# One maximum over 1024 keys instead of two over 512, and two banks of scores instead of three, in an attention kernel

## The chip, the cores and the metric

The kernel runs on one core of a Trainium2 chip. The metric is the time of one execution on the device in microseconds (us), as the median of several runs. The core has engines that run side by side and wait for one another by semaphores: TensorE (PE in the profile; its weight loads are PEld), VectorE (DVE), ScalarE (ACT), GpSimd (POOL) and SyncE (SP), which issues most of the transfers.

## What is computed

The input is 16 images of 128 channels by 32 x 32. Each image is normalised over its channels, read as 1024 tokens of 128 numbers, and goes through attention with 8 heads of size 16; the result is added to the image. Then the tokens go through a mixture of 16 experts of which each token takes two. The change touches the attention alone:

```
xs = reshape(_ln_c(x), (B, T, C))                 # B = 16, T = 1024, C = 128
q, k, v = per head xs @ Wq[h], xs @ Wk[h], xs @ Wv[h]
scores = einsum('bhtd,bhsd->bhts', q, k) * scale
att = softmax(scores, axis=-1)                    # over 1024 keys
out = einsum('bhts,bhsd->bhtd', att, v) ... @ Wproj + bproj
x = x + out
```

The softmax needs the maximum of each query's 1024 scores before the exponentials.

## The kernel before, in words

An image is worked on in 4 stages (2 groups of 4 heads, 2 halves of 512 queries). A stage has 32 slots, so an image has SLOTS = 128, numbered u in the code. In each slot TensorE does two things of the same size. `max_unit` (line 1265) multiplies 128 queries of one head by one half of the keys, 512 columns, into a bank of `ps_max`; a unit m has kh = m % 2 for the half of the keys, so an even unit and the odd one behind it belong to the same queries. VectorE takes the maximum over those columns (`take_max`, line 843), and in the first slot of the next stage `row_maxima` (line 850) joins the two halves. `split_m` writes the negated maximum as two bf16 parts (lines 864, 866, 869); TensorE turns them into rows (`rows_of_maxima`, line 1274), ScalarE copies these (`copy_m`, line 732), and a transfer puts them beside the queries. `score_unit` (line 1287) then computes the scores again, transposed, 128 keys by 512 queries with the maximum already subtracted, into a bank of `ps_score`; ScalarE takes the exponential (`exp_unit`, line 706) into `probs`; `weigh` (line 1306) multiplies by the values into `ps_pv`.

The maxima run LEAD = 46 units ahead of the scores, so before the first score stand 46 maxima, and in slot u TensorE does maximum u + 46 and score u. In an even slot the maximum comes first, in an odd slot the score, so that two scores stand next to each other. Weighing comes behind odd slots, by a table WEIGH_AT: at 1 and 3, then 7, 8, 9, 11 and every odd slot to 31 of a stage; none comes behind slot 5 of a stage.

PSUM has 8 banks of 512 fp32 columns. Three hold scores, three hold maxima (RING = 3), one holds the weighed values and one, `misc`, everything else. A unit may be written to a bank when its reader is through: score u waits for `exp_done`, maximum m for `max_taken`, both by `ring_free`, which means the third unit back. All orders are written out by hand and every engine takes its instructions in order. Beside the main work the slots hold the neighbouring images' other work: TensorE transposes the next image in slots 1 and 5, projects its queries and keys in 29, 41, 44, 48 and its values in 51 and 54; it projects the output of the last image in 13 and 17, transposes tokens in 22 and 24, does the logits in 36 and counts the tokens of each expert in 100. ScalarE copies what these give, and has `copy_xt` behind exponentials 2 and 6 (line 712), `copy_m` in slot 27 of each stage and `copy_rows` (line 749) behind exponentials 76 and 80. VectorE has `divide` in slots 4 to 7 of each stage (transposes and the division of the weighed values), statistics of the next image in 8 to 15 and of the last in 24 to 31, residual additions in 13 and 17, and steps of the choice of experts from 44 on. GpSimd adds the bias to the residual (line 544). SyncE stacks the parts of queries and keys for the next image (`stack`, line 325, twelve transfers) once score 63 is done; the maxima of the next image begin with unit 128, in slot 82, and wait for them. Images 1 to 14 are turns of a loop; the first and the last are written out.

Of the kernel before, what the change touches and what calls it, by code (L numbers as in the profile page):

```python
# [8 lines left out]
ALU = mybir.AluOpType  # L9
ACT = mybir.ActivationFunctionType  # L10
AX = mybir.AxisListType

P = 128
# [5 lines left out]
HALF = T // 2  # L19
# [4 lines left out]
STAGES = G * 2  # L24
UNITS = TB * HG
SLOTS = STAGES * UNITS
LEAD = 46
MSLOT = 26
RING = 3
PRING = 16  # L30
NORMS = 14
BUSY = (3, 4, 5, 6, 7, 18, 19, 20, 21)
# [9 lines left out]
STACK = 16 * len(Q_PART)  # L42
# [20 lines left out]
def wait(eng, sem, value):  # L63

    if isinstance(value, int) and value <= 0:
        return
    eng.wait_ge(sem, value)
# [10 lines left out]
def ring_free(n):  # L78


    return n - RING + 1 if n % SLOTS >= SLOTS % RING else n - SLOTS % RING + 1

# [6 lines left out]
def metaformer(nc, x, wq, wk, wv, wproj, bproj, wgate, w1, w2, out):  # L89
    ctx = ExitStack()  # L90
    with ctx:
        def sb(name, shape, dt=FP32):
            return ctx.enter_context(nc.sbuf_tensor("sb_" + name, shape, dt))

        def sem(name):
            return ctx.enter_context(nc.semaphore(name))
# [18 lines left out]
        qs, ks = stacks[:, 0], stacks[:, 1]  # L115
# [33 lines left out]
        blk_dest = arena_d[:, XR * ROWW + (WR + 2) * P:XR * ROWW + (WR + 2) * P + WR].bitcast(I32)  # L149
        o_t = sb("o_t", [P, HALF // 32, 32])  # L150
        o_rec = sb("o_rec", [P, HALF // 32])
        m_red = sb("m_red", [P, 2, UNITS])
        m_neg = sb("m_neg", [P, 2, HG * HG])
        m_rest = sb("m_rest", [P, HG * HG])
        m_parts = sb("m_parts", [P, HG, MPARTS, HG], BF16)
# [49 lines left out]


        banks = ctx.enter_context(nc.psum_tensor("banks", [P, 8, HALF], FP32))
        ps_score, ps_max = banks[:, 0:RING], banks[:, RING:2 * RING]
        ps_pv, misc = banks[:, 6], banks[:, 7]
        ps_h, ps_o, ps_xt = banks[:, 0:2], banks[:, 2:4], banks[:, 6:8]  # L210
        ps_y = banks[:, 0:4].rearrange("p (s h) t -> p s h t", s=2)
# [20 lines left out]
        v_placed = sem("v_placed")  # L232
        max_ready = sem("max_ready")
        max_taken = sem("max_taken")
        m_ready = sem("m_ready")
        m_split = sem("m_split")
        m_psum = sem("m_psum")
        m_copied = sem("m_copied")
# [599 lines left out]
        def _(dve):  # L838
            def take_max(b, m):

                s, u = m // UNITS, m % UNITS
                wait(dve, max_ready, SLOTS * b + m + 1)
                nc.vector.tensor_reduce(out=m_red[:, s % 2, u:u + 1], in_=ps_max[:, m % SLOTS % RING, :], axis=AX.X,  # L843
                                        op=ALU.max).then_inc(max_taken, 1)

            def row_maxima(b, s):
                k = STAGES * b + s
                wait(dve, max_taken, UNITS * (k + 1))
                wait(dve, m_split, 3 * (k - 1))
                nc.vector.tensor_reduce(out=m_neg[:, s % 2, :],  # L850
                                        in_=m_red[:, s % 2, :].rearrange("p (n s) -> p n s", s=2),
                                        axis=AX.X, op=ALU.max, negate=True).then_inc(m_ready, 1)

            def split_m(b, s, step):

                k = STAGES * b + s
                neg = m_neg[:, s % 2, :].rearrange("p (t h) -> p t h", t=HG)
                rest = m_rest[:, :].rearrange("p (t h) -> p t h", t=HG)
                wait(dve, m_split, 3 * k + step)
                if step == 0:  # L860
                    wait(dve, m_ready, k + 1)

                    wait(dve, m_psum, k)
                    nc.vector.tensor_copy(m_parts[:, :, 0, :], neg).then_inc(m_split, 1)
                if step == 1:
                    nc.vector.tensor_tensor(out=rest, in0=neg, in1=m_parts[:, :, 0, :],
                                            op=ALU.subtract).then_inc(m_split, 1)
                if step == 2:
                    nc.vector.tensor_copy(m_parts[:, :, 1, :], rest).then_inc(m_split, 1)
# [153 lines left out]
            for o in range(2):  # L1023
# [6 lines left out]
                                    op=ALU.subtract).then_inc(setup_v, 1)  # L1030
# [4 lines left out]
            for i in range(4):  # L1035
                o, half = i // 2, i % 2
# [4 lines left out]
                for level in (1, 2):  # L1041
                    dve.wait_ge(qk_parts, 5 * i + 2 * level - 1)
                    nc.vector.tensor_tensor(out=f, in0=f, in1=parts[:, o, level - 1, cols],
                                            op=ALU.subtract).then_inc(qk_parts, 1)
                    dve.wait_ge(qk_parts, 5 * i + 2 * level)
                    nc.vector.tensor_copy(parts[:, o, level, cols], f).then_inc(qk_parts, 1)
            for m in range(LEAD):
                take_max(0, m)
                if m == UNITS:
                    row_maxima(0, 0)  # L1050
                if 0 < m - UNITS < 4:
                    split_m(0, 0, m - UNITS - 1)

            def batch(b, first, last):
                for u in range(SLOTS):
                    m = u + LEAD
                    if not (last and m >= SLOTS):
                        take_max(b, m)
                    if m % UNITS == 0 and not (last and m > SLOTS):
                        row_maxima(b, m // UNITS - 1)  # L1060
                    if 0 < m % UNITS < 4 and not (last and m > SLOTS + 4):
                        split_m(b, m // UNITS - 1, m % UNITS - 1)
                    if 4 <= u % UNITS < 8 and not (first and u < UNITS):
                        divide(b, u // UNITS - 1, u % UNITS - 4)
                    if not last:
                        if 8 <= u < 16:
                            norm_stats(b + 1, 0, xt_copied, ln1_stats, u - 8)
                        if u == 17:
                            norm_means(b + 1, 0, ln1_stats)
                    if not first:  # L1070
                        if u == 13:
                            add_residual(b - 1, 0)
                        if u == 17:
                            add_residual(b - 1, 1)
                        if 24 <= u < 32:
                            norm_stats(b - 1, 1, tok_copied, ln2_stats, u - 24)
                        if u == 32:
                            norm_means(b - 1, 1, ln2_stats)
                        if u == 38:
                            choose(b - 1)  # L1080

                        if u == 44:
                            choice = choose_experts(b - 1)
                        if u >= 44 and u % 2 and u % UNITS not in BUSY:
                            next(choice, None)

            batch(0, True, False)
            with dve.Fori(1, B - 1) as b:
                batch(b, False, False)
# [30 lines left out]
            def three(t):  # L1120
# [9 lines left out]
                                        op=ALU.is_le))  # L1130
# [95 lines left out]
        def _(pe):  # L1226
# [29 lines left out]
            def max_unit(b, m):  # L1256

                s, u = m // UNITS, m % UNITS
                bb = b + s // STAGES
                g, half = s % STAGES // 2, s % 2  # L1260
                h, t, kh = u // 8, u // 2 % 4, u % 2
                if u == 0 and half == 0:
                    wait(pe, stacked[g], 192 * (bb + 1))
                wait(pe, max_taken, SLOTS * b + ring_free(m))
                nc.tensor.matmul(ps_max[:, m % SLOTS % RING, :], qs[0:STACK, g, h, half * HALF + t * P:half * HALF + (t + 1) * P],  # L1265
                                 ks[0:STACK, g, h, kh * HALF:(kh + 1) * HALF], start=True,
                                 stop=True).then_inc(max_ready, 1)

# [252 lines left out]
```

## Time and profile before

| | |
|---|---|
| median of 3 runs | 2675.8 us (2669.5 to 2680.6) |
| span of the profiled execution | 2676.3 us |
| TensorE matmuls | 2423.1 us busy, 91% |
| VectorE | 1997.1 us busy, 75% |
| ScalarE | 1511.7 us busy, 56% |
| GpSimd | 1187.5 us busy, 44% |
| mean granted clock of TensorE | 0.958 of full speed |

The profile is of one execution. Its span runs from the first to the last instruction. A busy share is a mean over stages with different limits: attention lasts to about 1942 us, the experts take the rest, and only in attention does the change have a part. A matmul's record is longer than the distance to the next one, since matmuls overlap; it is the distance between starts that tells the pace. In a timeline "x2" is two instructions in a row merged, and the bracket behind a row gives the idle time before it and what ended it.

### The profile page before, as it was taken

What the parts mean: (1) busy time and instruction counts of PE and PEld (TensorE: products, weight loads), DVE (VectorE), ACT (ScalarE), POOL (GpSimd) and SP (SyncE); (2) the same over time, 40 slices, a digit from 0 to 9 for tenths busy, and PEclk for the clock granted to TensorE, in tenths of its full rate; (3) what the DMA queues carried; (4) which work ended last, traced back from release to release, by engine and by line L of the source; (5) the groups of instructions that cost most, each with busy time, mean ns of one, the idle gap of its engine ahead of it and who ended that gap; (6) DMA issues with size and microseconds to landing.
All of it is one profiled execution on the core that took longest, in us unless ns stands there. A gap on an engine that the chain in (4) does not pass through costs nothing. (4 is left out here: it accounts for less than half of the span.)

```text
span 2676.3 us, 67960 instructions
## 1 busy us (share of the span) xinstructions
PE 2423.1 (91%) x18706; PEld 1203.4 (45%) x18706; DVE 1997.1 (75%) x4671; ACT 1511.7 (56%) x2881; POOL 1187.5 (44%) x1833
## 2 busy tenths in 40 slices
PE   3999999999999999999999999999928999999963
PEld 1333333333333333333333333333318999999962
DVE  6888888978888888888888898889624555555544
ACT  0576666766667666666666676667703444444420
POOL 4304536363544536263543637354264444444430
PEclk9999999999999999999999999999959999999985
DMA  2233222223232222223222222322062222222249
GB/s 44 33 52 55 51 42 59 34 58 53 57 59 48 59 34 58 41 58 65 53 51 42 58 34 58 63 47 57 10 179 62 63 63 63 63 64 63 63 117 286
DMA packets 142625, 168.55 MB, mean 63 GB/s; under 512 B 25214, under 2 KB 97284, under 8 KB 142370
## 3 DMA queue, kind: packets, MB, share of 16 engines
q1 hardware_dynamic: 125474, 131.08, 23.4%
q0 software_dynamic: 16896, 34.12, 4.5%
q8 instruction: 155, 2.54, 0.4%
q14 instruction: 100, 0.82, 0.1%
HBM read 60.66 MB, written 44.67 MB: 39 GB/s over the span
## 5 line engine op out<-in xcount | busy, mean ns | idle before, releaser
L843 DVE TENSOR_REDUCE sb_m_red<-banks 128x1 f32<-128x512 f32 x2048 | 1363.4, 684 | 252.4 <-PE banks L1265 240.1
L706 ACT ACTIVATE sb_arena_a<-banks 128x512 f32<-128x512 f32 x2048 | 1140.7, 596 | 581.3 <-PE banks L1287 570.0
L1265 PE MATMUL banks<-sb_arena_b 96*128 96x512 bf16 x2048 | 797.7, 394 | 54.4 <-issue 32.5
L1287 PE MATMUL banks<-sb_arena_b 104*128 104x512 bf16 x2048 | 661.1, 385 | 0.9 <-DMA sb_arena_b<-sb_m_row 0.9
L1306 PE MATMUL banks<-sb_arena_a,sb_arena_d 128*32 128x256 f32 x8192 | 661.5, 395 | 0.4 <-ACT sb_arena_a L706 0.4
L1265 PEld LDWEIGHTS banks<-sb_arena_b 96*128 96x128 bf16 x2048 | 199.1, 97 | 551.5 <-DVE sb_m_red L843 310.8
L689 POOL DMA_INDIRECT expert_out<-sb_arena_d x272 | 267.4, 983 | 306.3 <-DVE sb_arena_d L1169 265.3
L1306 PEld LDWEIGHTS banks<-sb_arena_a,sb_arena_d 128*32 128x32 f32 x8192 | 162.4, 108 | 438.6 <-issue 368.8
L1444 PE MATMUL banks<-sb_arena_d,sb_arena_c 128*128 128x128 f32 x2176 | 291.1, 277 | 40.6 <-ACT sb_arena_d L814 40.6
L634 POOL DMA_INDIRECT sorted_rows<-sb_rows,sb_place x256 | 248.0, 969 | 97.1 <-issue 90.1
L1453 PE MATMUL banks<-sb_arena_c 128*128 128x128 f32 x2176 | 287.4, 276 | 0.0
L1444 PEld LDWEIGHTS banks<-sb_arena_d,sb_arena_c 128*128 128x128 f32 x2176 | 265.7, 193 | 47.5 <-ACT sb_arena_d L814 47.5
L821 ACT ACTIVATE sb_arena_c<-banks 128x512 f32<-128x512 f32 x272 | 162.4, 597 | 219.9 <-PE banks L1444 219.9
L1287 PEld LDWEIGHTS banks<-sb_arena_b 104*128 104x128 bf16 x2048 | 202.8, 100 | 165.8 <-issue 37.4
L1453 PEld LDWEIGHTS banks<-sb_arena_c 128*128 128x128 f32 x2176 | 265.0, 192 | 0.0
L1171 DVE TENSOR_SCALAR sb_arena_d<-banks,sb_arena_d 128x128 f32<-128x128 f32 x272 | 95.2, 350 | 197.1 <-PE banks L1453 196.3
L1158 DVE COPY sb_arena_c<-sb_arena_a 128x512 f32 x272 | 114.7, 422 | 93.5 <-issue 93.5
L814 ACT ACTIVATE sb_arena_d<-banks 128x128 f32<-128x128 f32 x272 | 75.4, 277 | 145.7 <-PE banks L1436 145.7
L528 POOL TENSOR_TENSOR sb_qk_f<-sb_qk_f,sb_arena_c 128x512 f32<-128x512 f32 x120 | 138.8, 1157 | 21.2 <-POOL sb_arena_c L525 10.3
L585 POOL TENSOR_TENSOR sb_tmp<-sb_counts,sb_masks 128x128 f32<-128x128 f32 x16 | 7.3, 455 | 294.8 <-DVE sb_small L1006 288.3
L544 POOL TENSOR_TENSOR sb_res<-sb_res,sb_bias 128x1024 f32<-128x1024 f32 x16 | 37.8, 2361 | 198.2 <-DMA sb_res<-in_x_dram 198.2
L1161 DVE COPY sb_arena_c<-sb_arena_b 128x512 f32 x272 | 114.4, 421 | 0.1
(145 smaller groups left out, 1817.1 us busy)
## 6 DMA issues: line engine op xcount, KB each, us to landing
sb_arena_b<-sb_arena_c SPq DMA_DIRECT2D x384, 128.0 KB, 5.4
sb_arena_d<-sorted_rows SPq DMA_DIRECT2D x272, 66.0 KB, 1.8
sb_arena_a<-expert_out SPq DMA_DIRECT2D x32, 512.0 KB, 5.6
sb_x_in<-in_x_dram SPq DMA_DIRECT2D x16, 512.0 KB, 3.3
sb_res<-in_x_dram SPq DMA_DIRECT2D x16, 512.0 KB, 7.9
sb_x_all<-sb_res SPq DMA_DIRECT2D x16, 512.0 KB, 3.0
out_dram<-sb_arena_a SPq DMA_DIRECT2D x16, 512.0 KB, 3.7
expert_out<-sb_arena_d POOLq DMA_INDIRECT x272, 2.2
```

The costliest lines, as they stand in the source:

```text
L528: nc.gpsimd.tensor_tensor(out=f, in0=f, in1=parts[:, o, level - 1, cols], op=ALU.subtract).then_inc(qk_parts, 1)
L634: nc.gpsimd.indirect_dma_start(out=sorted_rows[:, :], out_offset=bass.IndirectOffsetOnAxis(ap=place[:, k, j:j + 1], axis=0), in_=rows[:, k ...
L689: nc.gpsimd.indirect_dma_start(out=expert_out[:, :], out_offset=bass.IndirectOffsetOnAxis(ap=blk_dest[:, s % WR:s % WR + 1], axis=0), in_= ...
L706: nc.scalar.activation(probs[:, u % PRING, :], ps_score[:, u % RING, :], ACT.Exp, scale=SCALE).then_inc(exp_done, 1)
L821: nc.scalar.activation(hid[:, s % 2, :], ps_h[:, s % 2, :], ACT.Relu).then_inc(hid_done, 1)
L843: nc.vector.tensor_reduce(out=m_red[:, s % 2, u:u + 1], in_=ps_max[:, m % SLOTS % RING, :], axis=AX.X, op=ALU.max).then_inc(max_taken, 1)
L1158: nc.vector.tensor_copy(w1_blk[:, s % WR, :], w1_all[:, bass.ds(e, 1), :].rearrange("p a h -> p (a h)")).then_inc(w1_copied, 1)
L1265: nc.tensor.matmul(ps_max[:, m % SLOTS % RING, :], qs[0:STACK, g, h, half * HALF + t * P:half * HALF + (t + 1) * P], ks[0:STACK, g, h, kh ...
L1287: nc.tensor.matmul(ps_score[:, u % RING, :], ks[0:STACK + MROWS, g, h, i * P:(i + 1) * P], qs[0:STACK + MROWS, g, h, half * HALF:(half + 1 ...
L1306: last = nc.tensor.matmul(ps_pv[32 * h:32 * h + 32, cols], v_pad[:, i, HG * g + h, :], probs[:, (4 * n + h) % PRING, cols], start=(i == 0 ...
L1444: last = nc.tensor.matmul(ps_h[:, s % 2, c * P:(c + 1) * P], w1_blk[:, s % WR, c * P:(c + 1) * P], blk_xt[:, s % 2, :], start=True, stop=True)
L1453: last = nc.tensor.matmul(ps_o[:, s % 2, 0:P], hid[:, s % 2, c * P:(c + 1) * P], w2_blk[:, s % WR, c * P:(c + 1) * P], start=(c == 0), sto ...
```

## The change

A pair of banks becomes the unit of the maxima. `ps_max` is now four banks, as two groups of two; the even unit of a pair writes the first bank of a group and the odd one the second, and one reduction goes over both, 1024 columns, and writes the negated maximum straight to `m_neg`. `m_red`, `row_maxima` and the semaphore `m_ready` are gone. `take_max` does nothing for an even unit. `max_taken` counts pairs, an even unit waits until the pair two back is taken, and an odd unit doesn't wait. To have four banks for maxima, the scores go from three banks to two, as RING is now 2, and `score_unit` waits for the second exponential back.

```diff
-RING = 3
+RING = 2
+PAIRS = SLOTS // 2
...
-        ps_score, ps_max = banks[:, 0:RING], banks[:, RING:2 * RING]
+        ps_score = banks[:, 0:RING]
+        ps_max = banks[:, 2:6].rearrange("p (g k) t -> p g k t", g=2)
...
             def take_max(b, m):
 
-                s, u = m // UNITS, m % UNITS
+                if m % 2 == 0:
+                    return
+                s, n = m // UNITS, m % UNITS // 2
+                if n == 0:
+
+                    wait(dve, m_split, 3 * (STAGES * b + s - 1))
                 wait(dve, max_ready, SLOTS * b + m + 1)
-                nc.vector.tensor_reduce(out=m_red[:, s % 2, u:u + 1], in_=ps_max[:, m % SLOTS % RING, :], axis=AX.X,
-                                        op=ALU.max).then_inc(max_taken, 1)
-
-            def row_maxima(b, s):
-                k = STAGES * b + s
-                wait(dve, max_taken, UNITS * (k + 1))
-                wait(dve, m_split, 3 * (k - 1))
-                nc.vector.tensor_reduce(out=m_neg[:, s % 2, :],
-                                        in_=m_red[:, s % 2, :].rearrange("p (n s) -> p n s", s=2),
-                                        axis=AX.X, op=ALU.max, negate=True).then_inc(m_ready, 1)
+                nc.vector.tensor_reduce(out=m_neg[:, s % 2, n:n + 1],
+                                        in_=ps_max[:, m // 2 % 2].rearrange("p k t -> p (k t)"), axis=AX.X,
+                                        op=ALU.max, negate=True).then_inc(max_taken, 1)
...
-                    wait(dve, m_ready, k + 1)
+                    wait(dve, max_taken, UNITS // 2 * (k + 1))
...
-                wait(pe, max_taken, SLOTS * b + ring_free(m))
-                nc.tensor.matmul(ps_max[:, m % SLOTS % RING, :], qs[0:STACK, g, h, half * HALF + t * P:half * HALF + (t + 1) * P],
+                if kh == 0:
+                    wait(pe, max_taken, PAIRS * b + m // 2 - 1)
+                nc.tensor.matmul(ps_max[:, m // 2 % 2, kh, :], qs[0:STACK, g, h, half * HALF + t * P:half * HALF + (t + 1) * P],
```

The two calls of `row_maxima`, in the maxima ahead of the first score and in the slots, are taken out as well.

## Rows read from the trace of the kernel before

**Rows 1.** Busy time in two stretches: PE, PEld, DVE, ACT, POOL, granted clock, DMA
```profile
56.00:84.00 28.00, 27.53 (x52) 5.11 (x51) 27.46 (x50) 0.59 (x1) 0.00 (x0) 1.00 0.08 16
84.00:1942.00 1858.00, 1810.76 (x13794) 637.94 (x13796) 1588.80 (x3375) 1263.35 (x2320) 840.04 (x1441) 0.98 0.26 50
```

**Rows 2.** The costliest groups of vector and scalar instructions
```profile
L843 DVE TENSOR_REDUCE sb_m_red<-banks 128x1 f32<-128x512 f32 x2048 | 1363.4, 684 | 252.4 <-PE banks L1265 240.1
L706 ACT ACTIVATE sb_arena_a<-banks 128x512 f32<-128x512 f32 x2048 | 1140.7, 596 | 581.3 <-PE banks L1287 570.0
```

**Rows 3.** Waits of TensorE from 200 to 1800 us: total, times, longest
```profile
PE banks L1265 <- issue: 32.5, 13, 2.7
PE banks L1265 <- DMA sb_arena_b<-sb_arena_c: 8.7, 13, 0.8
PE banks L1265 <- DVE sb_m_red L843: 2.5, 13, 0.2
```

**Rows 4.** Timeline of an ordinary pair: start, length, engine, line
```profile
1000.89 0.39 PE L1265 MATMUL banks<-sb_arena_b 96*128 96x512 bf16 x1
...
1001.12 0.60 PE L1287 MATMUL banks<-sb_arena_b 104*128 104x512 bf16 x2
1001.32 1.34 DVE L843 TENSOR_REDUCE sb_m_red<-banks 128x1 f32<-128x512 f32 x2
...
1001.55 0.38 PE L1265 MATMUL banks<-sb_arena_b 96*128 96x512 bf16 x1
1001.61 1.08 ACT L706 ACTIVATE sb_arena_a<-banks 128x512 f32<-128x512 f32 x2 [0.54 <-PE banks L1287]
...
1002.43 0.39 PE L1265 MATMUL banks<-sb_arena_b 96*128 96x512 bf16 x1
```

**Rows 5.** Timeline of slots 68 to 71 in one image, TensorE, then ScalarE
```profile
848.29 0.60 PE L1287 MATMUL banks<-sb_arena_b 104*128 104x512 bf16 x2
...
849.16 0.67 PE L1287 MATMUL banks<-sb_arena_b 104*128 104x512 bf16 x2
...
848.79 2.07 ACT L706 ACTIVATE sb_arena_a<-banks 128x512 f32<-128x512 f32 x4 [0.54 <-PE banks L1287]
```

**Rows 6.** Timeline of slots 76 to 79 in that image, TensorE, then ScalarE
```profile
854.59 0.60 PE L1287 MATMUL banks<-sb_arena_b 104*128 104x512 bf16 x2
...
855.09 0.60 ACT L706 ACTIVATE sb_arena_a<-banks 128x512 f32<-128x512 f32 x1 [0.54 <-PE banks L1287]
855.58 0.62 ACT L749 ACTIVATE sb_rows<-sb_rows 128x512 f32<-128x512 f32 x1
856.10 1.56 ACT L706 ACTIVATE sb_arena_a<-banks 128x512 f32<-128x512 f32 x3
```

**Rows 7.** Timeline of slots 64 to 87, SyncE, then the others
```profile
844.52 7.76 SPq L325 DMA_DIRECT2D sb_arena_b<-sb_arena_c  x12
...
859.81 0.39 PE L1265 MATMUL banks<-sb_arena_b 96*128 96x512 bf16 x1 [0.75 <-DMA sb_arena_b<-sb_arena_c]
...
860.85 2.36 POOL L544 TENSOR_TENSOR sb_res<-sb_res,sb_bias 128x1024 f32<-128x1024 f32 x1 [11.88 <-DMA sb_res<-in_x_dram]
...
861.54 1.71 DVE L864 CAST sb_m_parts<-sb_m_neg 128x16 bf16<-128x16 f32 x1
...
862.89 0.39 PE L1265 MATMUL banks<-sb_arena_b 96*128 96x512 bf16 x1
...
863.89 0.39 PE L1265 MATMUL banks<-sb_arena_b 96*128 96x512 bf16 x1 [0.18 <-DVE sb_m_red L843]
```

**Rows 8.** Groups of instructions by line and form, VectorE
```profile
L1194 DVE TENSOR_TENSOR sb_arena_a<-sb_arena_a 128x1024 f32<-128x1024 f32 x16 | 19.6, 1225 | 51.7 <-DMA sb_arena_a<-expert_out 51.7
```

**Rows 9.** Busy time and granted clock of a stretch behind a turn of the loop
```profile
899.95:903.50 3.55, 3.55 (x16) 1.44 (x17) 1.38 (x2) 1.08 (x2) 2.80 (x3) 0.50 1.04 201
```

**Rows 10.** Timeline of TensorE near the end of attention
```profile
1916.80 0.61 PE L1287 MATMUL banks<-sb_arena_b 104*128 104x512 bf16 x2
...
1917.91 0.60 PE L1287 MATMUL banks<-sb_arena_b 104*128 104x512 bf16 x2
```

More of the change, by code:

```diff
@@ L151, in metaformer @@
         o_rec = sb("o_rec", [P, HALF // 32])
-        m_red = sb("m_red", [P, 2, UNITS])
         m_neg = sb("m_neg", [P, 2, HG * HG])
@@ L234, in metaformer @@
         max_taken = sem("max_taken")
-        m_ready = sem("m_ready")
         m_split = sem("m_split")
@@ L1048, in _ @@
                 take_max(0, m)
-                if m == UNITS:
-                    row_maxima(0, 0)
                 if 0 < m - UNITS < 4:
@@ L1058, in batch @@
                         take_max(b, m)
-                    if m % UNITS == 0 and not (last and m > SLOTS):
-                        row_maxima(b, m // UNITS - 1)
                     if 0 < m % UNITS < 4 and not (last and m > SLOTS + 4):
```

## The prediction

> **What bounds the kernel now.** I write score u and maximum unit m for what `score_unit` and `max_unit` produce; a pair is two successive units, even first, and an image has 128 slots u. I read the stretches first [rows 1]: of the 1858 us in which the 16 images are attended to, TensorE is busy 1811. VectorE has 1589 busy us there, most of them maxima, and ScalarE 1263, most of them exponentials [rows 2]. The list of what TensorE waited for, from 200 to 1800 us [rows 3], says what its few idle microseconds are: 32.5 us in 13 turns of the loop over images, 8.7 us for 13 transfers of the stacked queries and keys, and 2.5 us for VectorE's maxima. The timeline of one ordinary pair [rows 4] shows the pace: even maximum at 1000.89, two scores from 1001.12, odd maximum at 1001.55, then the weighing of values, next even maximum at 1002.43, so 1.54 us a pair with matmuls back to back. VectorE needs 1.34 us of it, ScalarE needs 1.08. So TensorE sets the pace, and a cheaper maximum by itself moves nothing: a term of the sum is only a matmul that starts later, or no longer starts late.
>
> **What the change does to VectorE.** Two reductions of 512 columns (684 ns each, one after the other every 0.65 us or less, [rows 2, 4]) become one of 1024 columns, and the 64 short row maxima over m_red go, which were hidden. No row shows 1024 columns out of a bank. From above the price is two reductions of today, 1.37 us; from below it is 1.14, twice the 0.60 at which reductions follow each other when they run on end (27.46 us over 46, [rows 1]), less 0.06 for a fixed part that is paid once. The nearest row is the only vector instruction 1024 wide, 1.225 us [rows 8], against 0.684 for 512. I take 1.23. VectorE overlaps the end of one instruction with the next, so a pair costs it about 1.15 to 1.19 us where it cost 1.22 to 1.30. This relief is hidden behind TensorE, with two exceptions. Ahead of the first score 46 reductions run on end from 56 to 84 us [rows 1], 0.60 us apiece; 23 at 1.15 are 1.7 us less. And the cast at slot 83 stands for 1.71 us until GpSimd's addition of the bias ends (860.85 + 2.36 = 863.21, [rows 7]), and TensorE's odd maximum at 863.89 comes 1.00 us behind its even one at 862.89, against 0.66 in an ordinary pair [rows 4, 7]: 0.34 us lost. After the change the cast still ends at 863.2, but the next pair's reduction ends near 864.6, and what needs it is an even unit due at 864.44, itself later by what is added below. I take 0.33 us off a turn (the bound on the other side is nothing).
>
> VectorE also has less rope: today an even unit needs the third unit back, after the change the pair two back. That reduction can start 0.43 us after the odd matmul [rows 4], ends 1.23 later, and is needed 0.88 + 1.54 = 2.42 us after that matmul: 0.76 us to spare, plus 0.35 a pair. Slots 4 to 17 are the worst (two transposes, eight statistics, two residual additions: some 5.3 us of others' work in seven pairs worth 13.2 us of TensorE). With 1.15 to 1.19 a pair that is 13.5, within the slack; with 1.3 it is 14.4, past it.
>
> [...]
>
> **What the change does to the scores.** This is the dear part: the ring of scores goes from three banks to two, so score u waits for the exponential of u - 2 instead of u - 3. From the rows: an exponential starts 0.42 us after its score, 0.50 where u is a multiple of four (848.29 to 848.79, [rows 5]), lasts 0.60, the next one starts 0.49 after it, and TensorE starts 0.055 us after the one it waited for has ended (exponential 68 is over at 848.79 + 0.60 = 849.39, and score 71 starts at 849.16 + 0.67 - 0.38 = 849.45; that is today's wait, 0.06 over the 0.22 between neighbours). In an ordinary pair that starts at s, the odd exponential ends by s + 1.6; the odd score of the next pair is due at s + 1.76. It fits by 0.1 us. It doesn't in these slots:
> - After slot 68 no values are weighed, and score 70 follows 0.87 us behind [rows 5]. It now waits until 0.50 + 0.60 + 0.055 = 1.15: 0.28 us. Score 71 waits for exponential 69, 1.64 against 1.15 + 0.22: 0.27. Less today's 0.06: 0.49.
> - After the logits and after the token counts (slots 36 and 100) the odd score stands alone, and scores 39 and 103 come 0.87 behind 37 and 101, against 0.42 + 0.60 + 0.055 = 1.07: 0.20 each.
> - `copy_rows` in slots 76 and 80 stands between two exponentials [rows 6]: 77's starts at 856.10, 1.51 after score 76, and is over at 2.10; score 79 waits until 2.16, due at 1.76: 0.40. Score 83 the same: 0.40.
> - `copy_xt` in slot 2 delays exponential 3 to 1.39, so score 5 waits till 2.04, due at 1.76: 0.29. [...]
> The other copies of ScalarE (of queries, keys, values, tokens, counts) sit in slots where TensorE has work of 0.4 to 1.7 us of its own; they cost nothing, and with that cover gone each would cost up to 0.4.
>
> **Where a stall goes.** The even maximum in slot 82 pauses 0.75 us (8.7/13 = 0.67 in the mean) for the stacks of the next image [rows 3, 7]. SyncE issues those transfers when score 63 is done, from 844.52 on, and they land at a time that later matmuls don't move. So what is added between 64 and 82, 0.49 + 0.40 = 0.89, first eats the pause: 0.67 comes back. A turn of the loop thus costs 0.89 + 0.40 (score 83) + 0.40 (39, 103) + 0.19 - 0.67 - 0.33 = 0.88 us, and 14 turns 12.3. The first image has three bare pairs (0.49 each) and a larger wait at the cast, 1.1 in all; the last image 1.5. Behind it, with no maxima left, a pair takes 1.11 us (1916.80 to 1917.91, [rows 10]) with ScalarE on end; with two banks the odd score waits for the odd exponential before it, and a round of two pairs takes 2 x 0.65 of TensorE and 1.145 of waiting, some 1.24 a pair: 22 x 0.13 = 2.9.
>
> The sum: 12.3 + 1.1 + 1.5 + 2.9 - 1.7 = 16. The profiled execution spanned 2676.3 us, which is the median of the runs (2675.8) within 0.5. Forecast 2692 us.
>
> **The rivals.**
> 1. The two banks bind less than worked out, because ScalarE or the pause absorbs it all: only the gains at the cast and ahead of the first score are left, 14 x 0.33 + 1.7 = 6: 2670. For it: no score waits over 0.06 us today; against it: that very wait shows that the distance of 0.87 us is real and that TensorE starts 0.055 after the exponential.
> 2. The reduction over two banks costs as much as two. Then VectorE is over its slack from slot 4 to 17 and at the cast; at 1.30 a pair the seven pairs overrun by 14.4 - 13.2 - 0.8 = 0.4 us, at the cast 0.15 to 0.5 more, so 8 to 14 us over the images: 2703. It decides from some 1.3 us a reduction. Against it stands the vector addition of 1024 columns.
> 3. The pause in slot 82 absorbs nothing, since the transfers themselves shift with the scores: 14 x 0.67 = 9 more, 2701. Against it: the issue starts before slot 68.
> 4. VectorE, not TensorE, sets the pace after all: 1024 pairs at 0.075 to 0.15 us less, 77 to 154 us saved, near 2560. Against it: VectorE is through in 1.34 of 1.54 us [rows 4], and TensorE waited 2.5 us for it. [...]
> The clock is a spread on all: a turn leaves a half-clock stretch that is short or twice as long, worth about 1.4 us; 14 turns can shift by some 7 us.
>
> **How the numbers follow.** Chances: forecast 0.50, rival 1 0.20, rival 2 0.12, rival 3 0.12, rival 4 0.03, other 0.03. Half a per cent of 2675.8 is 13.4 us, about what a measurement tells from none. The forecast's own range is 2683 to 2701, some three fifths of it over 2689: 0.30 slower, 0.20 same. Rivals 2 and 3 are slower (0.24), rival 1 is the same with 0.16 and faster with 0.04 if the clock helps, rival 4 faster, of the other 0.01 each way. So faster 0.08, same 0.38, slower 0.54. The range takes in rivals 1 and 3 and most of 2: 2671 to 2706.
>
> **What would show it.** In the profile after: a reduction of 128x1024 near 1.23 us, 1024 times; ordinary pairs still 1.54 us; waits of the scores' matmuls or weight loads for the exponentials of 0.2 to 0.4 us in slots 39, 70, 71, 79, 83, 103; the wait for the stacks nearly gone; the cast at slot 83 still long with no late maximum behind it; pairs of 1.2 us and more at the end. A reduction of 1.3 us or more, waits of even maxima for VectorE in slots 8 to 18, or a pause for the stacks that stays at 0.7 would make me wrong.

## The result and the profile after

The changed kernel takes 2721.0 us (median of 4 runs, 2720.9 to 2721.5), against 2678.1 us of the kernel before run beside it: 1.0167 times as long, with an interval of 1.0145 to 1.0189. The forecast was 2692, with 2706 as its upper end. The direction was right and the size was not: of 43 us, 16 had been foreseen. The profiled execution spans 2718.9 us (before: 2676.3).

The page's groups of instructions that answer to [rows 2], and TensorE's two:

```profile
L848 DVE TENSOR_REDUCE sb_m_neg<-banks 128x1 f32<-128x1024 f32 x1024 | 1247.0, 1221 | 361.4 <-PE banks L1260 322.1
L706 ACT ACTIVATE sb_arena_a<-banks 128x512 f32<-128x512 f32 x2048 | 1144.9, 596 | 622.2 <-PE banks L1282 610.6
L1260 PE MATMUL banks<-sb_arena_b 96*128 96x512 bf16 x2048 | 794.8, 394 | 71.4 <-issue 50.5
L1282 PE MATMUL banks<-sb_arena_b 104*128 104x512 bf16 x2048 | 677.2, 386 | 14.0 <-ACT sb_arena_a L706 7.5
```

The reduction over 1024 columns takes 1.221 us, as priced (1.23), and VectorE spends 116 us less on maxima (1363.4 to 1247.0). None of it reaches the end. The exponentials are what they were. What is new is idle time of TensorE, and the list of its waits from 200 to 1800 us, read against [rows 3], says where (total us, times, longest):

```profile
PE banks L1260 <- issue: 50.5, 13, 4.4
PE banks L1260 <- DVE sb_m_neg L848: 6.1, 12, 0.6
PE banks L1282 <- ACT sb_arena_a L706: 5.8, 25, 0.2
...
PE banks L1260 <- DMA sb_arena_b<-sb_arena_c: 0.3, 1, 0.3
```

Three of these four had been looked for: scores now wait for exponentials, the pause for the stacks is gone (8.7 to 0.3), and VectorE holds TensorE up a little. The first line is the surprise: "issue" (time in which the engine waited for nothing that the profile shows) has grown from 32.5 to 50.5 us in the 13 turns of the loop over images, 1.38 us a turn, and no engine and no transfer is named for it.

**The scores' waits** are where they were forecast. TensorE's timeline of slots 76 to 83 (the pattern of [rows 6]; start, length, line):

```profile
873.22 0.38 PE L1282 MATMUL banks<-sb_arena_b 104*128 104x512 bf16 x1
...
873.83 0.39 PE L1282 MATMUL banks<-sb_arena_b 104*128 104x512 bf16 x1 [0.23 <-ACT sb_arena_a L706]
...
876.71 0.38 PE L1282 MATMUL banks<-sb_arena_b 104*128 104x512 bf16 x1
...
877.32 0.39 PE L1282 MATMUL banks<-sb_arena_b 104*128 104x512 bf16 x1 [0.23 <-ACT sb_arena_a L706]
```

Scores 78 and 79 start 0.61 us apart where neighbours have 0.22, and so do 82 and 83: 0.39 lost each. Read the distance of the starts and not the bracket: the record before lasts 0.38 where neighbours start 0.22 apart, so the bracket's 0.23 is too small.

**The turn of the loop**, image 6 to 7: the last two scores, the last weighing, then image 7's first maximum and first scores. First the kernel before (its last score and image 7's first), then the kernel after:

```profile
896.33 0.38 PE L1287 MATMUL banks<-sb_arena_b 104*128 104x512 bf16 x1
...
900.35 0.64 PE L1287 MATMUL banks<-sb_arena_b 104*128 104x512 bf16 x1
```
```profile
913.69 0.60 PE L1282 MATMUL banks<-sb_arena_b 104*128 104x512 bf16 x2
...
914.44 0.64 PE L1301 MATMUL banks<-sb_arena_a,sb_arena_d 128*32 128x256 f32 x8
919.29 0.60 PE L1260 MATMUL banks<-sb_arena_b 96*128 96x512 bf16 x1 [4.21 <-issue]
919.69 1.06 PE L1282 MATMUL banks<-sb_arena_b 104*128 104x512 bf16 x2
```

In the kernel after the last score stands at 913.91 (the second of the two that are merged at 913.69) and the next at 919.69, 5.78 us; in the kernel before it was 896.33 to 900.35, 4.02 us. This turn is one of the longer ones of the kernel after: in the mean of the 13 it is 5.38 against 3.99. What TensorE's sequencer does in between is the loop's comparing branch, the instruction that jumps back to the head of the loop (min/median/max ns, first of the kernel before, then of the kernel after):

```profile
L1418 PEldq COMPARE_BRANCH  x14: 82/3754/3981, 303.6 to 1844.3; - x14
```
```profile
L1413 PEldq COMPARE_BRANCH  x14: 83/4792/5362, 307.8 to 1882.9; - x14
```

The branch that falls through at the end of the loop takes 0.08 us, the 13 that jump back 3.65 to 3.98 in the kernel before and 4.60 to 5.36 in the kernel after. It also starts later, 0.02 to 0.07 us behind the start of the last score where it started 0.38 ahead of it. A branch that is taken lasts 44 times as long as the one that is not, or more (3.65 us against 0.083).

**The slots of the cast**, which answer to [rows 7] (SyncE's issue of the residual load, GpSimd's addition, VectorE's cast, TensorE's late maximum):

```profile
869.44 0.33 SPq L316 DMA_DIRECT2D sb_res<-in_x_dram  x1
...
878.36 2.36 POOL L544 TENSOR_TENSOR sb_res<-sb_res,sb_bias 128x1024 f32<-128x1024 f32 x1 [12.73 <-DMA sb_res<-in_x_dram]
...
879.10 1.65 DVE L862 CAST sb_m_parts<-sb_m_neg 128x16 bf16<-128x16 f32 x1
...
880.88 1.23 DVE L848 TENSOR_REDUCE sb_m_neg<-banks 128x1 f32<-128x1024 f32 x1
...
882.16 0.39 PE L1260 MATMUL banks<-sb_arena_b 96*128 96x512 bf16 x1 [0.58 <-DVE sb_m_neg L848]
```

The addition starts 8.92 us after the load's issue. In the kernel before it was 8.07 (860.85, [rows 7], less 852.78):

```profile
852.78 0.33 SPq L316 DMA_DIRECT2D sb_res<-in_x_dram  x1
```

The cast ends with the addition (880.75 and 880.72), the reduction behind it at 882.11, and the even maximum waits for that. It comes 2.19 us behind the even maximum before it (879.97), where an ordinary pair has 1.54 [rows 4]: 0.65 late.

The account of the two profiled executions, from the starts of the scores (mean of the 15 steps from one image to the next, after less before, us; the loop jumps back at 13 of them, so for a single jump the turn's entry is 15/13 as large):

| place | forecast | measured |
|---|---|---|
| scores 70, 71 | +0.49 | +0.43 |
| scores 39 and 103 | +0.40 | +0.43 |
| score 79 | +0.40 | +0.38 |
| score 83 | +0.40 | +0.35 |
| score 5 | +0.19 | +0.22 |
| pause for the stacks, slot 82 | -0.67 | -0.63 |
| late maximum behind the cast | -0.33 | +0.07 |
| turn of the loop, with slots 0 to 3 after it | 0 | +1.33 |
| the rest | 0 | -0.07 |
| sum over the images but the last | 13.4 (14 x 0.88 + 1.1 for the first image) | 37.8 (times 15) |

With the last image (5.7, forecast 1.5 + 2.9), the first score (0.4 later, forecast 1.7 earlier) and 1.4 us less behind the last score that makes the 42.6 us between the spans.

### The profile page after: what moved, and what is told of

The parts are those of the page before. It is cut to its first block and busy times, and to the rows that moved or that the text cites. A ratio compares the mean times of both kernels' runs of the same rounds, so it can differ in the third digit from the quotient of the medians.

```text
span 2718.9 us, 65024 instructions
## 1 busy us (share of the span) xinstructions
PE 2439.0 (90%) x18706; PEld 1195.2 (44%) x18706; DVE 1923.0 (71%) x3583; ACT 1516.3 (56%) x2881; POOL 1187.3 (44%) x1833
## 5 line engine op out<-in xcount | busy, mean ns | idle before, releaser
L848 DVE TENSOR_REDUCE sb_m_neg<-banks 128x1 f32<-128x1024 f32 x1024 | 1247.0, 1221 | 361.4 <-PE banks L1260 322.1
L1260 PE MATMUL banks<-sb_arena_b 96*128 96x512 bf16 x2048 | 794.8, 394 | 71.4 <-issue 50.5
L1282 PE MATMUL banks<-sb_arena_b 104*128 104x512 bf16 x2048 | 677.2, 386 | 14.0 <-ACT sb_arena_a L706 7.5
```

Source lines behind the costliest of these rows:

```text
L848: nc.vector.tensor_reduce(out=m_neg[:, s % 2, n:n + 1], in_=ps_max[:, m // 2 % 2].rearrange("p k t -> p (k t)"), axis=AX.X, op=ALU.max, ne ...
L1260: nc.tensor.matmul(ps_max[:, m // 2 % 2, kh, :], qs[0:STACK, g, h, half * HALF + t * P:half * HALF + (t + 1) * P], ks[0:STACK, g, h, kh * ...
L1282: nc.tensor.matmul(ps_score[:, u % RING, :], ks[0:STACK + MROWS, g, h, i * P:(i + 1) * P], qs[0:STACK + MROWS, g, h, half * HALF:(half + 1 ...
```

## The experiments

The times of a group of experiments were taken beside new runs of the kernel before, whose median was 2674.3 to 2678.5 us, so each is also given as a ratio to it. Two questions were open: is the ring of two score banks worth what the account says, and what lengthens the turn? TensorE's wait "issue" in 13 turns, from the same list as above, is given for each kernel; before has 32.5, after 50.5.

**Two score banks alone, three maxima.** The kernel before with the scores' ring cut, nothing else:

```diff
-        ps_score, ps_max = banks[:, 0:RING], banks[:, RING:2 * RING]
+        ps_score, ps_max = banks[:, 0:2], banks[:, 3:6]
...
-                wait(pe, exp_done, SLOTS * b + ring_free(u))
+                wait(pe, exp_done, SLOTS * b + ring_free(u, 2))
```

> The kernel before with two banks of scores, and three single maxima as they were. Theory A (the score ring is the whole cost: its waits in slots 39, 70, 71, 79, 83, 103, and at the turn of the loop score 127 now waits for exponential 125, so that TensorE's branch comes 0.4 us later and lasts 4.8 us where it lasted 3.8): 36 to 42 us slower than before, 2714 to 2720, branch near 4.8 us. Theory B (the longer turn comes with the merged maxima, from other programs of TensorE and VectorE): only the waits in the slots, 14 to 20 us slower, branch 3.8 us.

2687.6 us, 1.0037 (1.0022 to 1.0052) of the kernel before, 11 us more by the medians (2676.1). Issue 36.1. The waits for exponentials and the vanished pause are the same as in the kernel after, slot by slot; the late maximum behind the cast is gone (-0.39 a turn), and the turn costs 0.19 more, not 1.2. The ring's waits are what they were priced at, and the ring does not explain the turn. Theory A is out; the 14 to 20 us of Theory B were a little too much, since the late maximum goes and the stretches at half the clock are shorter here (51.2 us in all, 3.4 of them not behind a turn, against 61.4).

**Two score banks, four single maxima banks.** As above with all four other banks as a ring of maxima:

> Two banks of scores and four single banks of maxima, each with its own reduction of 512 columns: the change without the merge. Theory A: within 5 us of the changed kernel, some 2718, a bit less if the late maximum behind the cast at slot 83 goes away thanks to the fourth bank (13 times 0.5 us). Theory B: 14 to 20 us slower than before, 2695.

2687.4 us, 1.0042 (1.0026 to 1.0058), issue 36.1: without the merge the change costs 11 us and not 43, and a fourth bank of maxima is worth nothing.

**A late last score.** In the kernel before, score 127 alone waits as with two banks:

```diff
-                wait(pe, exp_done, SLOTS * b + ring_free(u))
+                wait(pe, exp_done, SLOTS * b + (ring_free(u) if u < SLOTS - 1 else u - 1))
```

> The kernel before, three banks of scores, with one wait more: score 127 waits for exponential 125, as it does with two banks; nothing else. Theory A: the branch comes 0.4 us later against score 127 and lasts 4.8 us, the turn is 1.4 us longer, 14 turns make 19 us: 2697. Theory B: no change, 2678.

2689.1 us, 1.0040 (1.0024 to 1.0056), issue 36.2. The branch starts 0.49 us later but is shorter (3.6 for 3.8), and the turn grows by 0.33. That is not the 1.4 that is sought. Its profiled execution spans 2682.0, so the 13 us of the medians are more than this place explains. Its stretches at half the clock last 75.1 us in all against 61.4 in the kernel before, and its other runs have a lower granted clock still (0.953 to 0.955 for 0.956); how much of the 13 us that makes is left open.

**The stacks issued later.** In the kernel after, the second group's transfers, which SyncE issues at the turn, are held until score 0 is done:

```diff
-                wait_apart(sp, sp_passed, scores_ready, SLOTS * (b - 1) + 2 * UNITS * (g + 1))
+                wait_apart(sp, sp_passed, scores_ready, SLOTS * (b - 1) + 2 * UNITS * (g + 1) + g)
```

> The changed kernel, in which SyncE issues the stacks of the second group of heads behind score 0 of the new image, where it issued them behind score 127 of the old one. If TensorE's branch is long because its instructions are fetched at the same time as those transfers run: branch 3.8 us or less, 14 times 1.4 us back, some 2700. If it is long for the fetches of the other engines, or for its own place in time: no change, 2720.

2719.5 us, 1.0150 (1.0125 to 1.0174), issue 50.9: the turn is as long. A collision with the stacks is out.

**What the trace shows at the turn.** The instruction fetches are transfers of their own. The rows of their queue (packets, MB, share), before, in the 4.5 us ahead of the last score of image 6, and then in the 4 us behind it:

```profile
q8 instruction: 1, 0.02, 1.6%
```
```profile
q8 instruction: 1, 0.02, 1.5%
```

After, the 4.5 us ahead of it hold no packet of that queue (or of any), and the 4 us behind it this:

```profile
q8 instruction: 2, 0.03, 6.0%
```

A 16 KB fetch that fell 4.2 us ahead of the last score now falls into the branch, next to another (in the kernel before the branch has a single one), and the two take four times the DMA time (6.0% against 1.5%). TensorE's program is 64 instructions shorter in each image of the loop, since odd maxima have lost their wait. Hence Theory C, in which the length of TensorE's program decides. Theory D has VectorE's program, which is shorter as well.

**TensorE's program made as long again.** The kernel after with a wait on odd maxima that is always met already:

```diff
-                if kh == 0:
-                    wait(pe, max_taken, PAIRS * b + m // 2 - 1)
+                wait(pe, max_taken, PAIRS * b + m // 2 - 1)
```

> The changed kernel in which TensorE's odd maxima carry the wait of their even neighbour again; it is always met, so it only gives TensorE's program its 64 instructions a turn back. Theory C (the turn is long because TensorE's program is shorter, so that the next 16 KB piece of instructions, which the kernel before fetches 4 us ahead of the branch, falls due during the branch and runs beside the fetch of the branch's target): the turn from the last pair to the next goes from 5.6 back to some 4.4 us, 14 x 1.2 = 17 us less, some 2703. Theory D (the length comes with VectorE's shorter program or the merged maxima as such): no change, 2720.

2697.3 us, 1.0079 (1.0057 to 1.0102): 24 us less than the kernel after, by 64 instructions more in each of the 14 images of the loop (the pages count 65920 for 65024). The ratios say the same, 1.0079 for 1.0167. The 17 us expected were the turn's alone; in the account it makes 16, and the late maximum behind the cast another 7. The branch is back at

```profile
L1412 PEldq COMPARE_BRANCH  x14: 83/3507/3690, 307.4 to 1860.1; - x14
```

issue at 34.6, and the first of the two fetches stands 2 to 3 us ahead of the last score again. The cast's slots are mended too:

```profile
860.30 0.33 SPq L316 DMA_DIRECT2D sb_res<-in_x_dram  x1
...
868.30 2.36 POOL L544 TENSOR_TENSOR sb_res<-sb_res,sb_bias 128x1024 f32<-128x1024 f32 x1 [11.83 <-DMA sb_res<-in_x_dram]
...
869.95 0.74 DVE L862 CAST sb_m_parts<-sb_m_neg 128x16 bf16<-128x16 f32 x1
...
870.82 0.39 PE L1259 MATMUL banks<-sb_arena_b 96*128 96x512 bf16 x1
```

The load is there 8.00 us after its issue, the cast starts 9.65 us after it (8.76 in the kernel before) and meets only the addition's end, and the maximum behind it is on time: -0.40 us a turn against the kernel before.

**The same length taken from the unmerged kernel.** Two score banks and four single maxima, the second experiment here, with the odd maximum's wait dropped and the even one's made to cover it:

```diff
-                wait(pe, max_taken, SLOTS * b + ring_free(m, 4))
+                if kh == 0:
+                    wait(pe, max_taken, SLOTS * b + m - 2)
```

> Two banks of scores and four single maxima as in the third run above, but the odd maxima lose their wait (the even one waits for both), so that TensorE's program is as short as in the changed kernel while VectorE's is that of before. Theory C: the turn grows from 4.4 to 5.6 us, 17 us slower than that run, some 2704. Theory D: as that run, 2687.

2719.0 us, 1.0161 (1.0138 to 1.0183), 32 us over that experiment, with no merge in it (67064 instructions for 67960). Issue 50.2, the addition 8.91 us behind the load's issue (868.99 to 877.90), and

```profile
L1419 PEldq COMPARE_BRANCH  x14: 83/4732/5292, 307.7 to 1880.9; - x14
```

Theory C holds in both directions. The 32 us are nearly twice the 17 expected: the turn makes 15 of them and the late maximum 7, and most of the rest lies in the first slots behind the turn; the stretches at half the clock last 64.9 us in all against 41.0 (6.8 of the 41.0 not behind a turn).

**VectorE's program made longer.** The kernel after, where VectorE also waits for each even unit, whose matmul is always done earlier (66159 instructions for 65024):

```diff
                 if m % 2 == 0:
+                    wait(dve, max_ready, SLOTS * b + m + 1)
                     return
```

> The changed kernel in which VectorE waits for the even units too, waits that are always met by the odd one behind; VectorE's program gets 64 instructions a turn back, TensorE's stays short. Theory C: no change, turn 5.6 us, 2720. Theory D: the turn shrinks towards 4.4 us, up to 17 us less.

2723.7 us, 1.0176 (1.0152 to 1.0199), issue 49.4. Theory D falls.

**All turns taken together.** The 13 kernels of this document have 13 turns each. The five with TensorE's short program (the kernel after, the later stacks, the unmerged one without odd waits, the longer VectorE program, and the cast as a reduction, which follows) have two packets of queue q8 in the branch in all 65 turns, and the branch lasts 4.5 to 5.4 us. The eight with the long one have a single packet in it in all 104, and it lasts 3.4 to 4.1. The packet that starts last takes 1.04 us in the median where it is alone and 2.14 where it has company, and in both groups the branch ends 1.50 us (median) after the last packet has landed. So what the branch gains in length is what its fetch gains.

The load of the residual goes by the place of such a fetch too, and here one kernel has both cases. The kernel with the shorter lead (below; long program) has a fetch 1.2 to 3.0 us behind the load's issue in ten turns, and the addition starts 7.9 to 8.1 us behind the issue. In its other three the fetch comes 4.9 to 5.0 behind, and the addition 8.9 to 9.0, as at this one:

```profile
1197.58 0.33 SPq L316 DMA_DIRECT2D sb_res<-in_x_dram  x1
...
1206.51 2.36 POOL L544 TENSOR_TENSOR sb_res<-sb_res,sb_bias 128x1024 f32<-128x1024 f32 x1 [12.73 <-DMA sb_res<-in_x_dram]
```

Over all 169 turns: fetch at 1.2 to 3.0 us, addition at 7.9 to 8.1 (81 turns); fetch at 3.9 to 5.1, addition at 8.4 to 9.0 (70 turns); fetch at 6.7 or later, addition at 7.75 to 7.95 (18 turns).

**The cast as a reduction.** Kernel after, the first step of `split_m` as a maximum over an axis of length one:

```diff
-                    nc.vector.tensor_copy(m_parts[:, :, 0, :], neg).then_inc(m_split, 1)
+                    nc.vector.tensor_reduce(out=m_parts[:, :, 0, :], in_=neg.unsqueeze(3), axis=AX.X,
+                                            op=ALU.max).then_inc(m_split, 1)
```

> The changed kernel in which the first part of the maxima is cast by a reduction over an axis of one element, where it was a copy with a cast. If the copy stands still because it shares a way to SBUF with GpSimd's addition of the bias: the 1.65 us cast at slot 83 falls to 0.2 us, TensorE's late maximum of 0.6 us in slot 88 goes, 13 times 0.5 to 0.6 us make 7 us less, 2713; unless the subtraction behind it, with two inputs in SBUF, now stands in its place, and then nothing changes. If the instruction is long for another reason: no change, 2720.

2717.9 us, 1.0155 (1.0132 to 1.0177), 3 us under the kernel after, which the two intervals don't tell apart. The two steps (busy us, mean ns), first of the kernel after, then of this one:

```profile
L862 DVE CAST sb_m_parts<-sb_m_neg 128x16 bf16<-128x16 f32 x64 | 38.9, 608 | 0.0
...
L864 DVE TENSOR_TENSOR sb_m_rest<-sb_m_neg,sb_m_parts 128x16 f32<-128x16 f32 x64 | 11.5, 180 | 2.2
```
```profile
L862 DVE TENSOR_REDUCE sb_m_parts<-sb_m_neg 128x16 bf16<-128x16 f32 x64 | 10.1, 158 | 0.0
...
L865 DVE TENSOR_TENSOR sb_m_rest<-sb_m_neg,sb_m_parts 128x16 f32<-128x16 f32 x64 | 33.7, 527 | 2.2
```

The reduction is not held by GpSimd: 15 of the 64 start while GpSimd's addition of the bias runs, and all 64 last 157 to 160 ns, where the cast had a mean of 608 ns. The subtraction behind it stands still in its place, with a mean of 527 ns against 180: in 14 of those 15 it lasts 0.54 to 1.51 us and ends 0.03 to 0.04 us after the addition, and 14 others last 0.67 or 0.68 us beside GpSimd's additions of line 528. The maximum after them gains 0.19 us a turn. Why the addition holds the cast and the subtraction and not the reduction isn't shown.

**A shorter lead.** The kernel before with the maxima of the next image two slots later (`BUSY` follows by two):

```diff
-LEAD = 46
+LEAD = 44
...
-BUSY = (3, 4, 5, 6, 7, 18, 19, 20, 21)
+BUSY = (3, 4, 5, 6, 7, 20, 21, 22, 23)
```

> The kernel before with the new image's lead shortened from 46 slots to 44, so that the even maxima that TensorE issues for the next image begin in slot 84 instead of 82 (and the slots at which VectorE is held back go two later with them). In the kernel before, TensorE pauses there for the transfers of the stacks, 8.7 us in 13 turns, and the odd maximum behind the cast is late, 0.34 us a turn. Theory P (both are a matter of when the first maxima fall due, and are real time on TensorE's path): the pause goes, and the cast, one pair later too, no longer stands behind the bias's addition; with 8.7 + 4.4 us of these and two maxima fewer ahead of the first score (1.2 us) this takes 14 us off, some 2664 us if the kernel before stands at 2678. The rival (the pause is only shifted: the maxima that are two slots later are made up for at the next turn, where the last of them then wait for VectorE): within 4 us of the kernel before. The turn of the loop should show a branch of 3.5 to 4 us on TensorE either way, since the number of TensorE's instructions is unchanged.

2664.9 us, 0.9968 (0.9956 to 0.9981) of the kernel before: 9.4 us faster than its 2674.3, and the fastest of all. TensorE's waits have no pause for the stacks any more:

```profile
PE banks L1265 <- issue: 31.4, 13, 2.7
PE banks L1265 <- DVE sb_m_red L843: 2.2, 5, 0.9
```

The pause is real time (-0.74, here and in what follows in the mean of the 13 turns). The late maximum went too (-0.28), but some lateness came up one pair on (+0.11), in one turn 1.1 us at once, so 14 us was too much.

**A shorter lead and two score banks**, and **the same with the merge and the long program**:

> The same shortened lead with two score banks (the maxima still single banks, three of them). Theory P of the prediction (the pause for the stacks ate 0.67 us a turn of what the ring of two scores adds): with the pause gone beforehand, the ring costs in full, 0.89 + 0.40 + 0.40 + 0.19 = 1.9 us a turn, 26 us in 14, with the ends 3 to 5 us more, so 27 to 31 us over the kernel with the shortened lead alone, near 2693. Rival (the waits of scores for exponentials are worth what two score banks cost with the long lead, since other work absorbs them): 9 to 13 us over it, near 2676.

> The kernel with the merged maxima and two score banks, with a wait that is already met on each odd maximum so that TensorE's program is as long as before, and with the shortened lead. It differs from the kernel with two score banks and the shortened lead by the merge of the reductions alone. Theory M (the merge has a price of its own, the 10 us by which it stood above two score banks with the long lead; an even maximum depends on the pair two back instead of the third unit back): 6 to 12 us above that kernel. Rival (the 10 us were the length of the half-clock stretches and not the merge): within 3 us of it, or under it by the two reductions fewer ahead of the first score.

The first takes 2687.6 us, 1.0044 (1.0028 to 1.0060), 22.6 over the kernel with the shorter lead alone, where with the long lead the same cut cost 11. That is far above the rival's 9 to 13, and below the 27 to 31 of Theory P. The slots' waits are those of the table, and the entry of the pause is 0.00 instead of -0.65: the pause had hidden that much. Most of what Theory P had too much comes from the clock, which it left as it was; the stretches at half of it last 37.5 us in all here and 51.2 without the cut. The second takes 2691.1, 1.0055 (1.0038 to 1.0072), 3.6 over the first, between Theory M (6 to 12) and its rival (within 3). With the long lead the merged kernel with the long program stood 10 us over the unmerged one. So the merged kernels stand perhaps 4 to 10 us above the unmerged ones, and whether the merge itself is the reason isn't shown. The half-clock stretches account for a part (in the profiled executions 44.4 against 37.5 us of them, and 54.6 against 51.2), one wait of 3.1 us for a transposed tile of GpSimd's for another; the rest isn't settled.

## Why the forecast was right and where it failed

**What bounds the kernel: right.** TensorE keeps the pace; 116 us less on VectorE left not a microsecond. The fourth rival is out.

**The price of the reduction: right** (1.221 for 1.23), and the second rival with it. But the gain ahead of the first score, 1.7 us, did not come. The reductions on end, VectorE's timeline of the kernel after:

```profile
56.87 3.58 DVE L848 TENSOR_REDUCE sb_m_neg<-banks 128x1 f32<-128x1024 f32 x3 [10.47 <-PE banks L1260]
...
69.78 7.14 DVE L848 TENSOR_REDUCE sb_m_neg<-banks 128x1 f32<-128x1024 f32 x6
```

Six take 7.14 us, so they start (7.14 - 1.22)/5 = 1.184 apart, where two of the old ones need 1.20. The forecast had 1.15: it took off 0.06 for a part that is paid once. No row shows that 0.06; it is an estimate, and [rows 1, 2, 8] give one of that size, 0.60 - (1.225 - 0.684). The runs show 0.02 in its place (1.20 less 1.184): on end each old reduction overlapped the next by 0.084 already (0.684 less 0.60), and the merged one does by 0.037. And the first starts 0.45 later, since it waits for two matmuls. Together that is 0.4 us later for the first score, where it had been put 1.7 earlier.

**The ring of two score banks: right**, place by place and within 0.06 us. The first rival is out. The distance of 0.87 us behind a slot without weighing, the 0.055 from an exponential's end to the matmul, and the copies between exponentials gave it, all read from the rows of before. No row or run shows the 0.19 for score 5: the rows give 0.29 for it, and what the half clock takes off was a guess. The runs showed 0.22 in its place, which is in part luck; the half-clock stretch behind a turn lasts 3.41 us at eight turns of the kernel before and 6.83 at five.

**The pause as a cushion: right.** -0.63 for -0.67, and with the pause removed beforehand the cut costs twice as much. The third rival is out.

**The late maximum behind the cast: wrong in the kernel after, by 0.40 a turn.** The step held GpSimd's addition fixed. It starts when the residual load has landed, and that took 0.85 us longer. The turns of the kernel after bear this out: where the load took 8.87 us or more, scores 87 and 88 stand 1.92 to 2.04 us apart, where it took 8.6 they stand 1.67 to 1.69, and where it took 8.4, 1.49 (1.32 is undisturbed). Where TensorE's program is as long as before, the maximum is on time, -0.39 and -0.40; there the merge is not what does it, since it is so with single maxima too: the slots before come later, and the cast meets less of the addition.

**The turn of the loop: the step that was missing.** The forecast took it over unchanged, 0 for +1.33 us a turn, 20 of the 27 us that it fell short (in the spans, 42.6 for 16). Its sum for a turn has no term for the jump at all. The change removes one instruction, a wait that is hidden, from every second maximum, and it was counted at nothing because nothing waited behind it. With its removal a 16 KB instruction fetch that had stood 4.2 us ahead of the last score (image 6) came to lie in the branch. That TensorE's program decides, and neither VectorE's nor the merge, is shown by the experiments that put the 64 waits back and take them away with little else changed. They used the same wait each time; no run made the program longer by another instruction, so the length and the presence of these waits are not told apart. That it is the second fetch which prolongs the branch is read from the packets' times, without exception in 169 turns; no run moved a fetch by itself. The later load goes by the place of a fetch among its packets rather than by the length as such: it is late in three turns of 13 with the long program and the shorter lead, and on time in one turn of 13 with the short program and the cast as a reduction (fetch 2.8 us behind the issue, addition 7.98). Why a fetch at that place delays it isn't shown.

**The end: nearly right.** The pairs with no maxima alternate as worked out:

```profile
1957.29 0.60 PE L1282 MATMUL banks<-sb_arena_b 104*128 104x512 bf16 x2
...
1958.39 0.85 PE L1282 MATMUL banks<-sb_arena_b 104*128 104x512 bf16 x2
...
1959.75 0.60 PE L1282 MATMUL banks<-sb_arena_b 104*128 104x512 bf16 x2
```

Two pairs take 2.46 us, 1.23 each, where [rows 10] have 1.11 and the forecast had 1.24; from score 82 to the last the image takes 2.8 us more (2.9). What comes before, 2.9 more, had been put at 1.5.

**The chances.** Added up from their parts they come to 0.55 for slower and 0.37 for same, a hundredth off those stated. The measured time lies above every rival's: none of the four had the turn in it, so that the outcome was "slower", the class that was forecast as the likeliest, owes more than half its size to a cause that the forecast didn't have.

So the change costs, by its parts: the ring of scores 11 us net of the pause, the shorter TensorE program 24 (32 without the merge), and some 4 to 10 that the merged kernels stand above the unmerged ones for reasons not settled.

## What to carry to other kernels

Count a removed or added instruction on the engine that sets the pace twice: for its time, and for what it does to the place of everything behind it. In this rolled loop 64 waits in a turn of TensorE's program decided whether one 16 KB instruction fetch fell into the jump back (104 turns) or two (65 turns, the branch about 1 us longer); compare the fetch queue's packets and the branch's record before and after, and try a few harmless waits before a change is judged. This ring, cut by one, could be priced to within 0.06 us a slot from the old trace, by the longest start-to-start of its reader in each slot; then look for a pause behind it that takes up what is added.

## What the runs showed of the hardware

- A jump back to the head of a body on TensorE takes 3.4 to 4.1 us with one 16 KB fetch in it (104 turns) and 4.5 to 5.4 us with two (65 turns); one that isn't taken takes 0.08 us.
- 64 instructions less on TensorE in each of 14 images, in a program that otherwise does the same, cost 32 us of 2687 (1.2%), and 24 in the merged kernel.
- A load of 512 KB landed 7.9 to 8.1 us after its issue where an instruction fetch came 1.2 to 3.0 us behind that issue, and 8.4 to 9.0 where it came 3.9 to 5.1 behind.
- A VectorE reduction over 1024 columns of two banks takes 1.221 us and follows the one before it in 1.184; over 512 columns 0.684 and 0.60.
- A cast of 128x16 numbers takes 0.16 us alone and 1.71 to 1.75 us beside GpSimd's addition in the turns of the kernel before; a reduction of the same tile takes 0.158 in the mean of all 64, and no more than 0.160 in the 15 beside that addition.
